# Linear attention's normalisation in five pieces instead of three, and two weight halves in other slots

## The reference

```python
xn = _layernorm(x)
x = x + _L0_gnn_ref(xn, ...) + _L0_mix_ref(xn[None], ...)[0]
x = x + _L0_ffn_ref(_layernorm(x)[None], ...)[0]

def _rgcn_conv(x, src, dst, etype, W, root, b):        # twice, relu between
    x_src = x[src]                                     # 41250 edges, 8 types
    seg = dst * num_rel + etype
    sums = segment_sum(x_src, seg); cnt = segment_sum(1, seg)
    mean = (sums / maximum(cnt, 1)).reshape(num_nodes, num_rel, -1)
    return einsum('nri,rio->no', mean, W) + x @ root + b

def _L0_mix_ref(x, W_qkv, W_proj, b_proj, gamma, beta, random_features):
    q_p = _phi(q, random_features)                     # exp(proj - norm_sq) / 16, 256 features
    k_p = _phi(k, random_features)
    kv = einsum('bhnm,bhnd->bhmd', k_p, v)
    out = einsum('bhnm,bhmd->bhnd', q_p, kv)
    k_sum = sum(k_p, axis=2)
    normalizer = einsum('bhnm,bhm->bhn', q_p, k_sum)[..., None]
    out = out / (normalizer + 1e-06)                   # the normalisation
    ... = layernorm(x + out @ W_proj + b_proj) * gamma + beta
```

## Time and profile before

| | us |
|---|---|
| three runs | 2957.41, 2967.86, 2965.63 |
| their median | 2965.63 |
| the profiled execution | 2959.68 |
| its span in the trace | 2957.9 |
| PE busy | 2637.5 (89%) |
| DVE busy | 1599.5 (54%) |
| POOL busy | 1266.3 (43%) |
| ACT busy | 778.0 (26%) |

### The profile page before, as it was taken

The page is one execution under the profiler, slowest core; times in us unless marked ns, Lnnn a source line. Parts: engine busy times, 40 slices in busy tenths (PEclk is TensorE's granted clock), DMA queues, the critical chain, the costliest instruction groups (busy, mean ns, idle before and its releaser), DMA issues.

```text
span 2957.9 us, 68470 instructions
## 1 busy us (share of the span) xinstructions
PE 2637.5 (89%) x24343; PEld 2008.1 (68%) x24343; DVE 1599.5 (54%) x3130; ACT 778.0 (26%) x1111; POOL 1266.3 (43%) x1376
## 2 busy tenths in 40 slices
PE   5998999978998859999999788986959999999989
PEld 4787888847676647888885667664537666666665
DVE  6576666654446654333333345546776646646631
ACT  2111121201222212211130121320135355365350
POOL 1685211147777745300005677773005164264271
PEclk9999999999999969999999899997979899999999
DMA  5233333459888966433236988998110000000013
GB/s 165 91 126 103 120 123 121 132 200 313 309 299 311 312 201 193 156 121 104 94 99 211 320 283 306 320 314 280 42 38 2 22 22 1 22 22 1 22 49 94
DMA packets 103837, 448.79 MB, mean 152 GB/s; under 512 B 20725, under 2 KB 21048, under 8 KB 99381
## 3 DMA queue, kind: packets, MB, share of 16 engines
q0 software_dynamic: 60352, 283.01, 28.5%
q1 hardware_dynamic: 40661, 123.20, 13.1%
q10 hardware_dynamic: 2592, 39.32, 3.9%
HBM read 361.50 MB, written 83.92 MB: 151 GB/s over the span
## 4 chain that ended last, share of the span: by engine, by line
PE 58%; DVE 17%; issue 8%; POOL 5%; DVEq 5%; DMA 4%; ACT 2%; POOLq 0%; ACTq 0%; SPq 0%
PE PS L1796 26%; PE PS L1806 4%; PE PS L2091 3%; PE PS L2174 3%; PE PS L1895 2%; PE PS L2157 2%; PE PS L1998 2%; DVE NMC L1716 2%; PE PS L1927 2%; PE PS L2158 2%; POOL GATA L732 2%; DVE RCP L1441 2%; POOL PL L769 2%; POOL ROW L732 1%; DMA MSG<-msg_table,SKEY 1%
## 5 line engine op out<-in xcount | busy, mean ns | idle before, releaser
L1796 PE MATMUL PS<-WHL,XT 128*125 (+1 forms) x2880 | 488.7, 329 | 6.3 <-DVE WHL L1132 4.2
L1796 PE MATMUL PS<-WHL,HT 128*125 (+1 forms) x2880 | 476.8, 328 | 13.2 <-DVE HT L1285 10.7
L1796 PEld LDWEIGHTS PS<-WHL,HT 128*125 (+1 forms) x2880 | 394.7, 138 | 91.6 <-DVE HT L1285 12.5
L1796 PEld LDWEIGHTS PS<-WHL,XT 128*125 (+1 forms) x2880 | 391.7, 138 | 82.6 <-issue 4.7
L769 POOL TENSOR_TENSOR PL<-PF 125x500 bf16<-125x500 f32 (+1 forms) x306 | 291.9, 981 | 252.6 <-ACT PF L984 248.8
L732 POOL DMA_INDIRECT GATA<-msg_table,SKEY x324 | 312.4, 964 | 144.0 <-issue 90.6
L1219 DVE SCALAR_TENSOR_TENSOR MSG<-PS,MSG 125x768 f16<-125x768 f32 x160 | 153.1, 957 | 353.0 <-ACT MSG L808 351.1
L808 ACT ACTIVATE MSG<-PS 125x768 f16<-125x768 f32 x160 | 129.6, 810 | 795.8 <-PE PS L1796 785.4
L732 POOL DMA_INDIRECT ROW<-msg_table,SKEY x216 | 213.7, 990 | 92.8 <-issue 60.5
L984 ACT ACTIVATE PF<-PS,QK 125x500 f32<-125x500 f32 (+1 forms) x360 | 212.8, 608 | 103.0 <-PE PS L2158 102.8
L2174 PE MATMUL PS<-V,PF 125*125 125x129 bf16 x1200 | 194.6, 258 | 26.3 <-POOL PL L769 24.2
(11 more groups left out here) (327 smaller groups left out, 4905.5 us busy)
## 6 DMA issues: line engine op xcount, KB each, us to landing
msg_table<-MSG SPq DMA_DIRECT2D x160, 336.0 KB
WST<-in_wg_dram ACTq DMA_DIRECT2D x16, 2304.0 KB, 10.3
WST<-in_wf_dram SPq DMA_DIRECT2D x7, 1536.0 KB, 6.2
KROW<-key_rows POOLq DMA_DIRECT2D x54, 192.0 KB, 3.8
WST<-in_wm_dram SPq DMA_DIRECT2D x6, 1152.0 KB
msg_table<-MSG SPq DMA_DIRECT2D x160, 39.0 KB
GATA<-msg_table,SKEY POOLq DMA_INDIRECT x324
ROW<-msg_table,SKEY POOLq DMA_INDIRECT x216
```

Of the source, the lines that this page charges most:

```text
L1796: ins = pe.matmul(PS[0:ROWS, b0 + h, 0:HALF], X[:, xp, k, bass.ts(t, ROWS)], panel_part(slot, wp, k, h), start=k == 0 and xp + wp == 0, st ...
```

## The change

The normalisation is cut into five pieces of 250 columns, D0 to D4. Between pairs they stand behind k0, k1, k2, v0 and v1 of the next pair. In the last pair of each layer D0 and D1 stand behind the eviction of o11, D2 and D3 behind that of o12, and D4 in the second slot after. Of the join's weights the high half goes from slot 77 to slot 75 and the low half to slot 81, behind the last sum. The three waits on `hf_made` count five pieces a pair.

```diff
@@ behind_groups
-                    if i > first and r in ("k0", "k1", "k2"):
-                        slots[grp].append((f"D{r[1]}", i - 1))
+                    if i > first and r in ("k0", "k1", "k2", "v0", "v1"):
+                        slots[grp].append((f"D{'k0 k1 k2 v0 v1'.split().index(r)}", i - 1))
+                    if i == first + LPAIRS - 1 and r in ("o11", "o12"):
+                        slots[grp] += [(f"D{n_}", i) for n_ in {"o11": (0, 1), "o12": (2, 3)}[r]]
                     columns += mix_columns(r)
                     if columns >= BEHIND * (grp - pieces + 1) and grp < AG - 1:
                         grp += 1
-            for c in range(3):
-                slots[grp + 1 + c].append((f"D{c}", first + LPAIRS - 1))
+            slots[grp + 1].append(("D4", first + LPAIRS - 1))
             if L == 1:
-                slots[grp + 4] += [("H", PAIRS), ("L", PAIRS)]
+                slots[grp + 2].append(("H", PAIRS))
+                slots[AG].append(("L", PAIRS))
@@ pair_out (SP)
-                    sp.wait_ge(S["hf_made"], 3 * (i + 1))
+                    sp.wait_ge(S["hf_made"], 5 * (i + 1))
@@ H (ACT)
-                                act.wait_ge(S["hf_made"], 3 * PAIRS)
+                                act.wait_ge(S["hf_made"], 5 * PAIRS)
@@ pair_results (DVE)
-                        c0, n = CHUNKS[int(r[1])]
+                        c0, n = 250 * int(r[1]), 250
@@ projection (PE)
-                        pe.wait_ge(S["hf_made"], 3 * PAIRS)
+                        pe.wait_ge(S["hf_made"], 5 * PAIRS)
```

## The result

The changed kernel takes 2974.6 us in the median of 20 runs, the kernel before 2965.4. The ratio of the two is 1.0035, with a 95% interval from 1.0023 to 1.0046, so +7 to +14 us, about +10: slower, by less than the 15 us that the prediction had put at the border of what a measurement can tell. The forecast of 2977 and its sum of +14.6 had the right sign and the right size, and the sum was 4 us too high. How much the four normalisations in the middle cost or win stayed inside the scatter.

A forecast was written before the change was run, and what follows sets the result against it. PE is busiest (89%), but waits for DVE's one-hots bound the aggregation ring. Terms 3.6 + 6.5 + 2.3 + 2.2 = +14.6 us give 2974.3 on the profiled run, 2980.2 on the median; forecast 2977, range 2961 to 2990.

The forecast's parts named there:

- sum of +14.6: Whole kernel: both last pairs, the low half and the four middle normalisations together add 14.6 us.
- Layer 1's last pair, +3.6: Layer 1's end: five pieces cost 12.8 us instead of 9.2, unhidden as DVE ends last; +3.6 us, range +2.5 to +4.
- Layer 2's last pair, +6.5: Layer 2's end: HOT 74 10.5 us later, 4.5 us of POOL slack, so the last gather comes 6.5 us later.
- The ring: Aggregation: DVE makes a HOT, PE multiplies and frees three groups back, POOL gathers; HOT delays beyond the slack reach layer's end.
- POOL can't issue faster than that, and it was issuing without a break: Layer 2's end: POOL takes some 5.0 us a group, so a late start of group 77 stays late until the last gather.
- The landing, put at 10.3 with ±2: Layer 2's last gather, beside HF's loads: time to land left at 10.30 us, with −2 to +2.
- The low half, +2.3: Join's weights on DVE, behind the last sum: nothing covers them ahead of the mark for PE's transposes; +2.3 us, between 1.8 and 2.62.
- The four in the middle, +2.2: Four normalisations between pairs: more DVE time against even spacing; +2.2 us in sum, range −1 to +6.
- The mechanism that was put for v0 and v1: Behind v0 and v1: eviction (0.75) and piece (2.32) follow the product, putting the HOT behind v1 2.1 us later.
- A: Layer 2's end: last gathers run into HF's loads and take 18 to 20 us, adding 8 to 10; chance 0.15.
- B: Middle normalisations: even spacing pays −12.6 us if DVE stays at or under 5.7 us; sum about 0; chance 0.2.

The follow-up runs named there:

- packed pieces: Four kernels with four of the last pair's five pieces in slot 72: the changed kernel, last pairs alone, low half back, and the changed kernel with HF's loads later (1.0043).
- the spread one: Changed kernel with the last pair's five pieces one each in slots 73 to 77, high half in slot 78; 0.9989 of the kernel before.
- the last pairs alone: Kernel before with only the last pair of each layer in five pieces, four in slot 72 and one in slot 74; 1.003 of the kernel before.
- low half back: Changed kernel with the join's weights, high and low half, back in slot 77; 1.0037 of the kernel before.
- slot 71: Kernel before with five middle pieces, last pair's three in slots 71 to 73 (D0 behind o10's eviction), HF's loads at group 79's read; 1.0034 of the kernel before.

## Why the prediction came out as it did

**Layer 1's last pair, +3.6.** Held. The four traces with the packed pieces have 55.0 to 55.3 us from HOT 72 to the last read. The trace of before has 53.5, but most with its three pieces have 51.8, so it is +1.8 or +3.5 by which of the two one takes; against the mean of all eight with three pieces in slots 74 to 76 +3.0.

**Layer 2's last pair, +6.5: mis-sized, 8 to 10.** The ring did what the sum said: HOT 74 later by 10.4, the first gather of group 77 by 5.7 to 6.5 us. The last gather was put 6.5 us later, and in the four traces with packed pieces it stands 7.6 to 10.0 us later. The step that was mis-sized rests on "POOL can't issue faster than that, and it was issuing without a break": a late start of group 77 did stay late, but it grew. A pause of 1.1 us more in group 79 stands in the traces of all four kernels with packed pieces and not in the spread one. Where the low half was left in slot 77 (the last pairs alone, and low half back), it also held a gather of group 80 for 2.2 us, with three others queued behind it. The prediction put the low half in slot 77 at nothing, since the gathers end later than DVE there, and did not see that it holds them. The changed kernel escapes this by its own move of the low half; in its trace 2.4 us were lost ahead of HOT 73 instead, in a stretch that the change doesn't touch. The landing, put at 10.3 with ±2, measured 9.3 to 10.8 in the three of them with the loads beside it.

**The low half, +2.3: right ahead of the mark, less in all.** It puts 2.5 us ahead of the mark in each of the four runs that have it there. Against that stands what it no longer holds up at the gathers, up to 2.2 us of issue, which the prediction did not have. Alone it was timed at 0.9994, and the trace shows 1.5 us back at the last read. And where the last read is early, JX's load beside HF's can end later still.

**What the sum left out.** With a late last read and HF's loads where they were, the projection follows after 12.1 and 12.2 us (last pairs alone, and low half back), with an early one after 13.4 to 17.0. So some 1 to 5 us of what layer 2's end costs come back. The prediction took only the small share of the low half for this and let the rest of the delay reach the end in full. From HOT 71 to the projection six traces with the old ends have 66.2 to 68.4 us (mean 67.2), the trace of after 78.2, or 75.9 without the 2.4 us lost ahead of HOT 73. That is +8.7 us where the sum had 6.5 + 2.3 = 8.8. So this total is right in part by luck: more was lost at the gathers and less reached the projection. With the +3.0 of layer 1 it makes some 12 us, and the timed +10 leaves about −1 for the middle, within a scatter that is larger than that.

**The four in the middle, +2.2.** Two timings of the same code gave −0.30% and +0.05%, and their intervals don't touch, so even the sign stays open. The traces of layer 1 stand at +2.7 and +1.0. The mechanism that was put for v0 and v1 is there in layer 1. The chain of waits in after, which answers to the earlier trace rows:

```profile
829.98 0.75 DVE VA L1423
...
830.83 1.72 DVE RCP L1443
...
834.63 0.42 DVE HOT L1367
...
836.47 0.75 DVE VA L1423
...
837.32 1.72 DVE RCP L1443
...
841.10 0.43 DVE HOT L1367
```

Eviction and piece follow each other, and a group takes 6.5 us where, by the prediction's estimate, PE needs 5.7. HOT 38 stands at 58.9 us behind HOT 28 instead of 57.2. Rival B's condition, that DVE stay at or under 5.7, was missed by 0.8, since the idle time of 1.2 isn't filled: it is behind the multiply, here too. The granted clock at the first v product of the second pair is 1.00 in this trace, where it was 0.83. But of the eight traces with five pieces there only four have 1.00 in the 10 us ahead of it and four 0.83, so that the even spacing keeps it up is not shown.

**Rivals.** A did not happen as put: no last gather took over 12 us to land, 10.76 in the changed kernel. B fell for the changed kernel. With the last two pieces in another place, D3 and D4 behind K03, some 5 of its 12.6 us came, though not in the stretch of layer 1 where they were expected.

What stays open is the pause of 1.4 us in group 79, and how much the middle brings in layer 2, where a stretch scatters by 10 us from trace to trace (98.5 to 108.6 from HOT 28 to 46 in all fourteen).

## What to carry to other kernels

Work on an engine that feeds a ring should be spread so that no gap exceeds the ring's slack: the same five pieces cost nothing measurable in five slots and some 13 us more when four stood in one. Idle time in a timeline is ahead of the instruction that waits, so a piece fills it only if it is put ahead of that instruction (behind K03, ahead of kv0's eviction), not behind it (slot 71). And ask of each piece of work what it holds up while it runs, on other engines too: the low half had no price in the prediction where it stood, but there it held a gather for up to 2.2 us, about as much as it costs in front of the mark.

## What was not expected of the hardware

An indirect gather takes POOL 0.95 us to issue. In the fourteen traces 88 of the 9072 gathers take more than 2 us (2.15 to 3.31), and they are exactly those that start more than 0.1 us after the start and before the end of a pair's or the join's low half on DVE, a SCALAR_TENSOR_TENSOR with two tensors read from SBUF that takes 2.6 us. Each of them ends 0.81 to 0.83 us behind it. A multiply of the normalisation, which also reads two tensors from SBUF, can stretch a gather to 1.40 us. A reciprocal of 3.28 us, which reads one, never does: 180 gathers start beside one, and all take 0.94 to 0.96.

A last gather of layer 2 that landed in 4.94 us alone took 8.5 to 11.7 us beside 3.2 MB of loads (10.30 in the kernel before, of which some 2.2 are the hold). And executions of one kernel scatter by 0.7% (20 us), so that an interval from 12 runs that excluded no change ([0.9955, 0.9985]) was not borne out by 12 more of the same code.
